# Attention and expert layers on one core: each head's scores from 64 rows instead of 128, two heads side by side

## The reference, cut to what matters

```
xn = layernorm(x)
q = rope(xn @ wq);  k = rope((xn @ w_down) @ wk_up);  v = (xn @ w_down) @ wv_up   # 16 heads of 8
scores = q k^T / sqrt(8); allowed where page(key) <= page(query), a page is 32 tokens
s = softmax(scores) v @ wo
logits = silu(xn @ rw1 + rb1) @ rw2 + rb2;  two of 8 experts, weights by softmax
y = xn + sum_e w_e (silu(xn @ ew1_e + eb1_e) @ ew2_e + eb2_e)                      # hidden 256
out = x + s * silu(y)
```

## Time and profile before

| | us |
|---|---|
| median of three runs | 665.55 (663.73 to 666.62) |
| profiled execution, its span | 663.7 |
| its own time beside the span | not given apart; the lowest run is 663.73 |
| PE busy | 607.3 (92%) |
| PE weight loads busy | 448.6 (68%) |
| DVE busy | 467.0 (70%) |
| ACT busy | 354.4 (53%) |
| one round, start to start | 76.4 |

### The profile page before, as it was taken

How to read it: one execution, slowest core, us unless ns; L and a number is a source line. 1 busy time by engine, 2 the same in 40 slices (tenths; PEclk the granted TensorE clock), 3 DMA queues, 4 the chain that set the end, 5 groups by cost and what they waited for, 6 DMA issues and landing times.

```text
span 663.7 us, 12438 instructions
## 1 busy us (share of the span) xinstructions
PE 607.3 (92%) x4116; PEld 448.6 (68%) x4116; DVE 467.0 (70%) x1199; ACT 354.4 (53%) x507; POOL 18.6 (3%) x20
## 2 busy tenths in 40 slices
PE   2569999999999999999999999999999999999895
PEld 1448855787567865678557875788656885578643
DVE  6677866787568866798667865698757875687502
ACT  2123456643766347754576438653576445763573
POOL 0000000000000100001000000001000000000000
PEclk9758999999999989999999999999999998999999
DMA  5810002100120002200021001200021001200000
GB/s 170 210 43 2 3 13 61 27 1 19 38 60 1 18 1 49 46 1 18 21 51 25 1 18 45 50 1 18 1 67 28 2 17 25 51 22 2 19 1 16
DMA packets 21798, 20.93 MB, mean 32 GB/s; under 512 B 4545, under 2 KB 14450, under 8 KB 21778
## 3 DMA queue, kind: packets, MB, share of 16 engines
q1 hardware_dynamic: 21778, 20.67, 12.9%
HBM read 5.45 MB, written 2.10 MB: 11 GB/s over the span
## 4 chain that ended last, share of the span: by engine, by line
PE 70%; DVE 13%; issue 12%; ACT 2%; SPq 1%; DMA 1%; DVEq 0%; POOLq 0%; POOL 0%; ACTq 0%
PE bank L500 15%; PE bank L580 10%; PE ring L517 7%; PE ring L562 7%; PE bank L446 5%; PE bank L447 5%; PE bank L448 5%; PE bank L517 5%; DVE row_max L861 5%; PE ring L565 2%; DVE acc L908 2%; PE ring L566 2%; PE bank L462 1%; ACT probs L683 1%; PE bank L478 1%
## 5 line engine op out<-in xcount | busy, mean ns | idle before, releaser
L683 ACT ACTIVATE probs<-ring 128x768 f32<-128x768 f32 (+1 forms) x192 | 158.9, 880 | 79.7 <-PE ring L562 48.8
L861 DVE TENSOR_REDUCE row_max<-ring 128x2 f32<-128x256 f32 (+1 forms) x192 | 152.3, 819 | 13.1 <-PE ring L517 13.0
L643 ACT ACTIVATE eh<-bank,bias_cols 128x512 f32<-128x512 f32 x128 | 87.8, 686 | 136.9 <-PE bank L448 134.9
L500 PE MATMUL bank<-ew_sb,eh 128*128 128x128 f32 x1024 | 125.8, 276 | 2.4 <-DVE x_lo L786 2.4
L500 PEld LDWEIGHTS bank<-ew_sb,eh 128*128 128x128 f32 x1024 | 120.1, 192 | 5.6 <-issue 3.8
L517 PE MATMUL ring<-k_head,q_stack 108*128 108x256 f32 (+2 forms) x384 | 93.4, 344 | 12.3 <-DVE row_max L861 11.2
L517 PEld LDWEIGHTS ring<-k_head,q_stack 108*128 108x128 f32 x384 | 66.7, 194 | 37.0 <-DVE row_max L861 24.8
L580 PE MATMUL bank<-probs,v_cols 128*32 128x512 f32 (+3 forms) x1024 | 88.0, 442 | 0.4 <-ACT probs L683 0.4
L908 DVE SCALAR_TENSOR_TENSOR acc<-bank,gate_w,acc 128x128 f32<-128x128 f32 x224 | 63.1, 345 | 32.3 <-PE bank L500 32.1
L856 DVE TENSOR_REDUCE row_max<-bank 128x1 f32<-128x128 f32 (+3 forms) x128 | 58.9, 487 | 32.6 <-PE bank L517 31.7
L562 PE MATMUL ring<-q_stack,k_head 128*128 128x512 f32 (+1 forms) x256 | 71.8, 395 | 3.5 <-ACT probs L683 3.5
(11 more groups left out here) (115 smaller groups left out, 659.4 us busy)
## 6 DMA issues: line engine op xcount, KB each, us to landing
k_stack<-roped_hi SPq DMA_DIRECT2D x64, 64.0 KB, 2.0
q_stack<-roped_hi SPq DMA_DIRECT2D x64, 64.0 KB, 2.0
k_stack<-roped_lo SPq DMA_DIRECT2D x32, 64.0 KB, 2.0
q_stack<-roped_lo SPq DMA_DIRECT2D x32, 64.0 KB, 2.0
out<-out_sb SPq DMA_DIRECT2D x8, 256.0 KB, 2.3
x_all<-in_L_attn_x SPq DMA_DIRECT2D x4, 448.0 KB, 6.9
probs<-in_L_ffn_ew SPq DMA_DIRECT2D x1, 1024.0 KB, 5.8
q_stack<-neg_rows SPq DMA_DIRECT2D x32, 16.0 KB
```

The costliest lines, as they stand in the source:

```text
L500: last = mm(ps[:, t * E:(t + 1) * E], eh[:, s % EH_RING, t * P:(t + 1) * P], ew2_sb[:, e, f, :], start=(f == 0), stop=(f == HALVES - 1))
L643: nc.scalar.activation(eh[:, s % EH_RING, :], wide[s % 2][:], ACT.Silu, bias=bias_cols[:, s:s + 1]).then_inc(hidden_done, 1)
L683: nc.scalar.activation(probs[:, n % 2, r:r + 2, lo:T], ring[:, r:r + 2, lo:T], ACT.Exp, scale=SCALE).then_inc(exp_done, 1)
L861: V.tensor_reduce(row_max[:, g, i, 2 * pair:2 * pair + 2], ring[:, 2 * (m % 2):2 * (m % 2) + 2, 0:(i + 1) * P], AX, ALU.max).then_inc(max_ ...
```

## The change

- A head's operands are 36 to 38 rows and lie in one half ("strip") of the 128 rows: even heads in rows 0 to 63, odd heads in rows 64 to 127. A strip is 12 mask rows, three parts of 8 rows, 2 rows of maxima. A score matmul uses one strip; the two heads of a pair use both. No `k_head` products are needed: the steps `heads` and `act_head` go.
- `q_strip` and `k_strip` have two halves (batch number modulo 2), so a batch's operands are filled while the one before is in use. A fill goes through DRAM: two writes of 512 KB (`hi_rows`, `lo_rows`), a wait for them, then twelve reads of 128 KB. The constant rows are put in place once, by twelve DMAs, before the first fill; DVE's cast of the expert weights waits for them, since they are staged in `ew1_hi`.
- Negated maxima also go through DRAM: one write of 16 KB, a wait, two reads.
- The bank maxima (`max0`) are now those of group 3 of the same batch instead of group 0 of the next. All sixteen stand in steps 1 to 5 of stage two. The ring maxima are of groups 0 to 2.
- Second layers 6 and 7, the read-out of 5, the expert bias, projection 1 and two of the four `neg_max` move to stage two.
- The loop over batches is written out. Several tiles share memory (`r_act` with `o_t`, the output is added in place in `gated`).

```diff
-    max_steps = (1, 1, 2, 2, 2, 2, 2, 2, 2, 2, 1, 2, 1, 1, 1, 0)
-    layer2_at = {4: 0, 6: 1, 7: 2, 9: 3, 11: 4, 13: 5, 15: 6}
+    max_steps = (1, 2, 2, 2, 1, 2, 1, 2, 1, 2, 1, 2, 1, 2, 1, 1)
+    layer2_at = {4: 0, 6: 1, 8: 2, 10: 3, 12: 4}
...
-             4: [("weights", 0), ("neg_max", 0)], 5: [("out_rows", 2), ("negate", 1)],
-             6: [("weights_t", 0)], 7: [("out_rows", 3)], 8: [("neg_max", 1), ("stats", 0)], 9: [("out_cols", 0)],
-             10: [("negate", 2)], 11: [("project", 0)], 12: [("neg_max", 2), ("norm", 0)],
-             15: [("negate", 3)]}
+             4: [("weights", 0), ("negate", 0)], 5: [("out_rows", 2), ("neg_max", 0)],
+             6: [("weights_t", 0)], 7: [("out_rows", 3)], 8: [("stats", 0)], 9: [("out_cols", 0), ("negate", 1)],
+             11: [("project", 0), ("neg_max", 1)], 13: [("norm", 0)]}
...
-    return seq + [("layer2", NE - 1), ("neg_max", 3), ("proj", 0), ("expert_bias", 0), ("proj", 1)]
+    return seq + [("negate", 2), ("layer2", 5), ("proj", 0)]
...
-    before_pv = {5: [("heads", 0)], 8: [("heads", 1)]}
-    after_pv = {0: [("proj", 2), ("split", 0), ("proj", 3)], 1: [("split", 1), ("stack", 0)], 4: [("stack", 1)],
-                7: [("stack", 2)], 10: [("stack", 3)], NSTEP: [("values", 0), ("negate", 0)]}
-    for n in range(NMAX0):
-        at = 6 + n * 6 // NMAX0
-        (after_pv if n * 6 % NMAX0 >= 12 or at == 8 else before_pv).setdefault(at, []).append(("max0", n))
+    before_pv = {0: [("proj", 1), ("neg_max", 2)], 1: [("max0", 0), ("max0", 1)]}
+    after_pv = {1: [("proj", 2), ("split", 0), ("proj", 3)], 2: [("split", 1), ("stack", 0), ("max0", 2), ("max0", 3)],
+                3: [("max0", n) for n in range(4, 8)], 4: [("max0", n) for n in range(8, 12)],
+                5: [("max0", n) for n in range(12, 16)] + [("negate", LAST)], 6: [("layer2", 6)],
+                7: [("neg_max", LAST)], 8: [("layer2", 7)], 10: [("expert_bias", 0)], NSTEP: [("values", 0)]}
...
+                half, u, rows = b % 2, (GH * g + r) // 2, slice(STRIP * (r % 2), STRIP * (r % 2) + STOP0)
+                return mm(ps[:, 0:width], q_strip[rows, half, u, i * P:(i + 1) * P], k_strip[rows, half, u, 0:width],
                           start=True, stop=True)
...
             def maxima(b, g, jobs):
-                sp.wait_ge(neg_rows_ready, NG * b + g + 1)
-                sp.dma_start(q_stack[MAX0:MAX0 + MAX_SLOT, g, :].bitcast(F32),
-                             neg_rows[:, g, :]).then_inc(neg_in[g], 16)
+                made, sent = NG * b + g + 1, 16 * (NG * b + g + 1)
+                sp.wait_ge(neg_rows_ready, made)
+                sp.dma_start(max_rows[g].rearrange("p u s t -> (p u s) t"), neg_rows[:, g % NEG_RING, :]).then_inc(neg_out, 16)
+                sp.wait_ge(neg_out, sent)
+                for strip in (0, 1):
+                    base = STRIP * strip + STOP0
+                    sp.dma_start(q_strip[base:base + 2, b % 2, 2 * g:2 * g + 2, :].bitcast(F32),
+                                 max_rows[g, :, :, strip]).then_inc(neg_in[g], 16)
```

More of the change, by code:

```diff
@@ L341, in run @@
             first_round(do)
-            with eng.Fori(1, B - 1) as b:
+            for b in range(1, B - 1):
                 middle_round(do, b)
@@ L410, in store @@
             def store(b, _, jobs):
                 sp.wait_ge(out_ready, b + 1)
-                sp.dma_start(out[b].rearrange("(t p) e -> p t e", p=P), out_sb[:]).then_inc(stored, 16)
+                sp.dma_start(out[b].rearrange("(t p) e -> p t e", p=P), gated[:]).then_inc(stored, 16)
             sp.wait_ge(prep_dve, 2)
+            for strip in (0, 1):
+                base = STRIP * strip
+                for tile, w, row, first, n in ((q_strip, 0, base, 0, NMASK), (k_strip, 1, base, 0, NMASK),
+                                               (k_strip, 1, base + STOP0, ONES, 2)):
+                    for half in (0, 1):
+                        sp.dma_start(tile[row:row + n, half].bitcast(F32), rows_r[first:first + n, w, :].bitcast(
+                            F32).unsqueeze(1).to_broadcast([n, H // 2, T])).then_inc(rows_in_place, 16)
@@ L540, in max_scores @@
                 for r in range(2):
-                    last = row_scores(ring[:, 2 * (m % 2) + r, :], g, i, 2 * pair + r)
+                    last = row_scores(ring[:, 2 * (m % 2) + r, :], b, g, i, 2 * pair + r)
                 last.then_inc(max_full, 1)
@@ L876, in router @@
                     ffn_weights()
-            def heads(b, g, jobs):
-                if isinstance(b, int) and b == 0 and g == 0:
-                    dve.wait_ge(s_const, 16 * (2 + NG))
-                dve.wait_ge(k_in[g], 48 * b + 48)
-                for r in range(GH):
-                    last = ts(k_head[:, GH * g + r, :], k_stack[:, g, :], hmask[:, r:r + 1], None, ALU.mult)
-                last.then_inc(heads_ready, 1)
             def pv(b, n, jobs):
@@ L935, in _ @@
                   "logits": logits,
[L936 removed]
+                  "top": top_two, "weights": weights, "max0": max0, "max": max_scores, "negate": negate, "pv": pv,
                   "values": values, "layer2": layer2, "expert_bias": expert_bias,
                   "out_rows": out_rows, "project": project}
[L940 to L949 removed]
+            run(dve, do)
         @block.gpsimd
@@ L965, in project @@
                 pool.wait_ge(gated_ready, b + 1)
-                if later(b, 1):
-                    pool.wait_ge(stored, 16 * b)
-                G.tensor_tensor(out_sb[:], gated[:], x_all[:, b, :, :], ALU.add).then_inc(out_ready, 1)
+                G.tensor_tensor(gated[:], gated[:], x_all[:, b, :, :], ALU.add).then_inc(out_ready, 1)
             run(pool, {"stats": row_stats, "project": project})
-PER_LINKS = sum({"top": 1, "weights": 2, "out_rows": 1, "stats": 3, "negate": 1}.get(s[0], 0)
-                for s in STAGE_B + STAGE_C)
 _INS = ["L0_attn_x", "L0_attn_wq", "L0_attn_w_down", "L0_attn_wk_up", "L0_attn_wv_up", "L0_attn_wo",
```

189 lines of the change are left out of this document (83 added, 106 removed).

## The result

The changed kernel took 877.17 us in the median of four runs (871.56 to 882.14), the kernel before 666.09 (663.73 to 666.92). The ratio is 1.3169 (95% interval 1.311 to 1.3229). The forecast of 707 had the right sign and was 170 us too low; 877 lies outside its range. The profiled execution took 882.14 us, its span is 880.3.

A forecast was written before the change was run, and what follows sets the result against it. PE leads, with DVE or ACT close behind in each stage. 80 + 39.5 + 6 x (43.5 + 39.5) + 43.5 + 46.2 for the end gave 707 us; own range 688 to 732, 8-in-10 range 648 to 735.

The forecast's parts named there:

- stage two: Scores, exponentials, probabilities by values of a batch: 28.7 us before, forecast 39.5 us, bounds 34 to 43.
- Fills: Next batch's twelve reads in the second stage: issued from near 11 to 23 us, needed 15 us later, costing nothing.
- surcharge: Second stages: more waits could halve the granted clock every round, 12 us on top, 719; no case of its own.
- Opening: Before batch 0's scores: constant fills 7.2 us, first fills landing near 43, scores at 80 instead of 90.6.
- Stage one: Router to last first layer: 47.7 us before, forecast 43.5, DVE 33.9; bounds 38.5 to 47.5.
- visits: Switches from 128 to 64 rows and back in the first stage: 16 at 0.42 us, 6.7 us a round.
- Strips side by side: Two heads' score matmuls at once halve their time: 3.8 us saved in the first stage, 4.6 in the second.
- serialized rival: Score matmuls of a pair run one after another: 48 us more, 755 in all; chance 0.06.
- free rival: 64-row and 128-row matmuls mix without emptying the array: 644 us; chance 0.25 with nearly free switches or a faster walk.
- DVE's pauses: Second stage, steps 3 to 5: four bank maxima in a row hold PE 1.35, 1.65 and 2.0 us.
- walk: Step-by-step timing of the second stage: steps 3, 4, 5 start at 9.3, 12.9, 16.0 us from the first scores.
- DRAM round trip: Group 3's negated maxima, wanted by scores 9 in the second stage: PE waits 2.0 us, bounds 0 to 4.

The follow-up runs named there:

- e1: The changed kernel with the six upper-strip fill reads issued behind group 3's negated maxima, the other six left where they were: 813.40 us.
- f8: The changed kernel with GpSimd issuing the twelve fill reads, in an order in which neighbours write different partitions: 797.79 us.
- e5: e1 with every score matmul contracting all 128 rows, unused rows zeroed, no pairs side by side, exponential's scale 0.001: 785.78 us.
- e8: e1 with the bank maxima of steps 3 to 5 placed two before and two after the probabilities by values: 799.47 us.
- f2: The kernel before with its stage-two scores and bank maxima contracting 64 rows, order and waits unchanged, exponential's scale 0.001: 690.07 us.
- e4: The kernel before with its ring maxima contracting 64 rows instead of 108, one after another: 695.62 us.
- e9: The changed kernel with its twelve fill reads issued by GpSimd instead of SP: 870.20 us.
- f3: The changed kernel with the twelve fill reads still on SP, reordered so that neighbours in the queue write different partitions: 842.21 us.
- e2: The changed kernel with the negated maxima's write and two reads issued by GpSimd instead of SP, fills staying on SP: 879.98 us.

## Why the prediction was wrong, step by step

- **Fills.** The failed step: "they are off SP's queue by then, and the next first stage needs them 15 us later: nothing". It priced the reads by their issue and by the landing time of single DMAs, and not by the time in which 1.5 MB gets into eight partitions at a time. Ahead of the maxima, that time is 9.6 us a round (11.6 of wait in each of the seven rounds with a fill, instead of 2.0); e1 takes off 11.0 us of stage two with the clock that goes with it, f8 11.3 without moving a step. The earlier trace rows had a hint: 64-KB fills to 32 partitions and a mean of 44 GB/s over the stage.
- **Clock.** The surcharge of "8 x 1.5 = 12 us on top" failed by size. Once the fill waits are gone (e1), stage two is still 8.4 us above 39.5; full rows take back 4.2 of them (e5), spreading the maxima 2.0 (e8). What the remaining 2 to 4 us are isn't shown. I had tied the clock to pauses only, since the one row of before with 0.50 followed one; that narrow matmuls let it fall after pauses which full rows survive, and keep it down (f2), was no part of it.
- **Opening.** "12 constant fills x 0.6 = 7.2" came from issues of another shape and was 24 us; the fills forecast to land near 43 let the first ring maxima start at 80.17. Together they are the 37 us by which these were late; the 37 us from there to the scores (44 less 7.7 is 36.3, to be exact) came out at 37.9.
- **Stage one.** Right in the sum, 42.5 for 43.5, with DVE 33.3 for 33.9. Its parts were off: visits cost 0.24 to 0.29 us, not 0.42 (e4 and the rows below), so 16 are 4 to 5 us, not 6.7. Whether pairs are worth more than the visits they cost (my terms: 3.8 against 6.7) isn't settled. e5, without either, has 44.4 in the mean, 2 us more, but its first stages also wait 1.5 to 2.4 us each for the late fill, and only two of these six have a clock of 1.00. Those two take 43.5 and 43.9 us with waits of 2.0 and 2.4 in them; the 41.5 that are left of either would make the visits dearer than the pairs by about a us.

```profile
344.79:388.29 43.50, 38.54 (x251) 32.63 (x249) 33.26 (x93) 16.82 (x27) 2.30 (x2) 1.00 0.05 10
```
```profile
348.39 0.47 PE L529 MATMUL ring<-k_strip,q_strip 128*128 128x256 f32 x2 [1.98 <-issue]
```

The visits in the changed kernel:

```profile
179.48 0.40 PE L454 MATMUL bank<-x_lo,ew_hi 128*128 128x512 f32 x1
179.81 0.50 PE L524 MATMUL ring<-k_strip,q_strip 36*128 36x256 f32 x4
180.24 0.50 PE L452 MATMUL bank<-x_hi,ew_hi 128*128 128x512 f32 x1
181.13 0.38 PE L524 MATMUL ring<-k_strip,q_strip 36*128 36x256 f32 x2
```

- **Strips side by side.** Right. Two matmuls of 256 columns lie in one record of 0.38 us, four take 0.43 from start to start, less than their 0.48 in a row, although a change of shape is in it. The serialized rival is out. The free rival is out, too: leaving the 64-row shape costs 0.19. (Its own sum was a us a round too high: 39.5 less 20 x 0.2 is 35.5, not 36.5.)
- **DVE's pauses.** The walk holds to 0.3 us up to the start of step 4, at full clock. It ends there because it was made at full clock.
- **DRAM round trip.** 2.0 us forecast; 1.3 to 3.1 in e1, f8 and the last batch. Right wherever no fill is under way.

The 8-in-10 range failed with three terms that had no spread of their own: "nothing" for the fills had no upper end, the opening had none either (its 38 us alone would have passed the range), and the clock's price was taken from one stage of the kernel before.

## What to carry to other kernels

A DMA is off the path when it has landed, not when it is issued: price a fill by its bytes over the rate into the partitions that it writes, and look at what small DMA is issued behind it, whatever its queue. Reads into few partitions should be spread, so that those in flight together use other engines and other partitions; either one alone gained 7 and 35 us here (e9, f3), both together 79 (f8). A matmul that contracts a third of the rows takes as long for its columns as one on all rows (f2's usual second stage has 28.9 us, the kernel before 28.5). Where such matmuls are most of the work and PE has short waits between them, look at the granted clock: here it halved, and two heads side by side did not win that back.

## What was not expected of the hardware

- Eight partitions take in 60 to 66 GB/s, from eight DMA engines (share 0.55) and from sixteen (1.09, e9); with the reads in flight on different partitions sixteen bring 116 GB/s (f8).
- A 16-KB write to DRAM behind 1.5 MB of reads took 11.5 us issued by SP (the changed kernel), and 10.0 issued by GpSimd (e2).
- PE busy for 36.00 of 36.00 us at a granted clock of 0.50, with scores on 64 rows (f2), where the same sequence on 128 rows, with the same waits ahead of it, had 1.00.
- Entering the 64-row shape costs 0.10 us, leaving it 0.19 (e4).
